# Queries of two batches projected in one matmul over 512 columns, in every second batch's turn

## The reference, cut to what matters

```python
q = jnp.einsum('oc,bct->bot', Wq, target) + bq[None, :, None]
k = jnp.einsum('oc,bcs->bos', Wk, source) + bk[None, :, None]
v = jnp.einsum('oc,bcs->bos', Wv, source) + bv[None, :, None]
dot = jnp.einsum('bhdt,bhds->bhts', q, k) / math.sqrt(HEAD_DIM)   # 16 heads of 8
mask = target_mask[:, :, :, None] * source_mask[:, :, None, :]
dot = mask * dot - (1.0 - mask) * NEG
amap = jax.nn.softmax(dot, axis=-1) * mask
out = jnp.einsum('bhts,bhds->bhdt', amap, v)
```

## Time and profile before

| | |
|---|---|
| median of 3 runs (lowest, highest) | 509.4 us (509.39, 510.41) |
| profiled execution, its own time | 509.36 us |
| its span, first to last instruction | 507.6 us |
| granted TensorE clock, mean of the span | 0.997 of full speed |
| PE busy, share of the span | 474.1 us, 93% |
| DVE busy | 381.3 us, 75% |
| ACT busy | 244.9 us, 48% |
| POOL busy | 230.1 us, 45% |
| the sixteen L1325 reduces of a batch, each | 0.68 us |

### The profile page before, as it was taken

One profiled execution on the slowest core, in us unless ns is written; L12 is line 12 of the kernel. 1 busy time (PEld: TensorE's weight loads), 2 busy tenths in 40 slices (PEclk: granted clock), 3 DMA queues, 4 the chain that ended last, 5 costly groups with the idle time before them and its releaser, 6 DMA issues. The chain is left out here.

```text
span 507.6 us, 10286 instructions
## 1 busy us (share of the span) xinstructions
PE 474.1 (93%) x3384; PEld 259.3 (51%) x3384; DVE 381.3 (75%) x765; ACT 244.9 (48%) x461; POOL 230.1 (45%) x319
## 2 busy tenths in 40 slices
PE   2998999998999999999999998998999999999993
PEld 2663664854733633343343333333445647788882
DVE  4989889899888789999999999998465633333321
ACT  2761232332232078889999998787412010233331
POOL 3736434154755355867677763213010660042433
PEclk9999999999999999999999999999999999999998
DMA  7750175002775116566566655300022224378843
GB/s 237 216 176 0 43 166 89 2 0 62 186 195 150 54 57 174 147 171 184 162 163 172 171 153 147 84 5 5 1 94 77 74 94 166 120 185 195 192 112 41
DMA packets 67256, 59.96 MB, mean 118 GB/s; under 512 B 10048, under 2 KB 62256, under 8 KB 67216
## 3 DMA queue, kind: packets, MB, share of 16 engines
q1 hardware_dynamic: 63712, 55.24, 39.6%
q0 software_dynamic: 3072, 4.21, 4.9%
q10 hardware_dynamic: 432, 0.00, 0.0%
HBM read 38.90 MB, written 22.50 MB: 121 GB/s over the span
## 5 line engine op out<-in xcount | busy, mean ns | idle before, releaser
L1325 DVE TENSOR_REDUCE MX<-psum 128x2 f32<-128x512 f32 x256 | 162.1, 682 | 10.0 <-PE psum L1190 8.4
L1374 ACT ACTIVATE HP<-psum 128x512 f32<-128x512 f32 x224 | 122.1, 602 | 28.9 <-PE psum L1205 26.4
L1190 PE MATMUL psum<-QKA 60*128 60x256 bf16 x512 | 81.3, 273 | 7.1 <-DVE MX L1325 5.6
L1205 PE MATMUL psum<-QKA 60*128 60x256 bf16 x512 | 81.1, 273 | 1.5 <-DMA QKA<-max_scr 1.0
L1291 PE MATMUL psum<-HP,VP 128*32 128x256 f32 x1024 | 81.8, 391 | 0.3 <-issue 0.2
L602 PE MATMUL psum<-space_a,space_w 128*128 128x512 f32 x160 | 73.1, 602 | 1.9 <-DVE HP L629 1.9
L1190 PEld LDWEIGHTS psum<-QKA 60*128 60x128 bf16 x512 | 31.6, 94 | 63.8 <-DVE MX L1325 44.6
L1966 POOL DMA_INDIRECT out_x<-OE,to_u x16 | 24.9, 1557 | 62.6 <-ACT OE L2001 60.1
L602 PEld LDWEIGHTS psum<-space_a,space_w 128*128 128x128 f32 x160 | 29.0, 190 | 36.5 <-issue 31.0
L2089 PE MATMUL psum<-XT,WE 128*128 128x256 f32 (+1 forms) x192 | 44.0, 379 | 0.9 <-ACT XT L1985 0.9
L199 PE MATMUL psum<-space_a,wsh 128*128 128x512 f32 (+1 forms) x96 | 43.6, 598 | 0.3 <-PEq L1497 0.3
(11 more groups left out here) (207 smaller groups left out, 767.3 us busy)
## 6 DMA issues: line engine op xcount, KB each, us to landing
QKA<-stack_scr SPq DMA_DIRECT2D x32, 480.0 KB, 4.5
stack_scr<-PARTS SPq DMA_DIRECT2D x32, 192.0 KB, 2.1
WE<-in_W SPq DMA_DIRECT2D x16, 352.0 KB, 4.0
stack_scr<-PARTS SPq DMA_DIRECT2D x32, 128.0 KB, 2.0
XD<-dispatched SPq DMA_DIRECT2D x8, 258.0 KB, 3.9
X<-in_x SPq DMA_DIRECT2D x4, 512.0 KB, 5.8
CTX<-in_ctx SPq DMA_DIRECT2D x4, 512.0 KB, 8.2
MB<-in_mask SPq DMA_DIRECT2D x16, 128.0 KB, 3.3
```

What stands on the lines that cost most here:

```text
L1190: return pe.matmul(to[:, tt * T:(tt + 1) * T], QKA[rows, k, 0, h, tt * P:(tt + 1) * P], QKA[rows, k, 1, h, :], start=True, stop=True)
L1205: return pe.matmul(to[:, (m % 2) * T:(m % 2 + 1) * T], QKA[rows, k, 1, h, st * P:(st + 1) * P], QKA[rows, k, 0, h, :], start=True, stop=True)
L1325: dve.tensor_reduce(MX[:, par, head_of(n), :], src[:, :].rearrange("p (a s) -> p a s", a=2), axis=AX.X, op=ALU.max).then_inc(a_red, 1)
L1374: act.activation(PT[:, i % 2, st, 2 * half:2 * half + 2, :].rearrange("p j t -> p (j t)"), TBK3[THIRDS[m]], ACT.Exp).then_inc(a_exp, 1)
```

## The change

Z3 gets two sides, and a new tile QS of two sides stands between the bank and QK. In turns 0 to 9, only the even turns have a query step: in step 3 POOL normalises batches b+6 and b+7, in step 6 PE projects both in one matmul over 512 columns into the whole of bank 7, in step 7 ACT takes 512 columns out. `act_qk` no longer waits until the rests of the batch before are done (a_rest), but until the masking of the batch two before has read its side of QS (a_masked). `pool_query` reads QS in place of QK. The transpose of maxima waits for a_x3 in every turn in addition to a_qk. The prologue keeps its single projections, in the new tiles.

```diff
-            Z3 = sbp("Z3", [P, T])
+            Z3 = sbp("Z3", [P, 2, T])
+            QS = sbp("QS", [P, 2, T])
...
+            def pe_proj_two(pe, g, k, to=bank[7]):
+
+                pe.wait_ge(a_z3, GB * g + k + 2)
+                pe.matmul(to[:, :], wq[:], Z3[:, :, :].rearrange("p b t -> p (b t)"), start=True, stop=True).then_inc(a_proj, 2)
...
             def act_qk(act, b, of=bank[7]):
 
                 act.wait_ge(a_proj, b + 1)
-                if later(b):
-                    act.wait_ge(a_rest, 2 * b)
-                act.activation(QK[:, 0:T], of[:, 0:T], ACT.Identity, bias=bqk[:, 0:1]).then_inc(a_qk, 1)
+                if b > 1:
+                    act.wait_ge(a_masked, b - 1)
+                act.activation(QS[:, b % 2, :], of[:, 0:T], ACT.Identity, bias=bqk[:, 0:1]).then_inc(a_qk, 1)
+
+            def act_qk_two(act, b, of=bank[7]):
+
+                act.wait_ge(a_proj, b + 2)
+                act.wait_ge(a_masked, b)
+                act.activation(QS[:, :, :].rearrange("p b t -> p (b t)"), of[:, :], ACT.Identity,
+                               bias=bqk[:, 0:1]).then_inc(a_qk, 2)
...
-                pool.tensor_tensor(QK[:, 0:T], QK[:, 0:T], MB[:, k, :], ALU.mult).then_inc(a_masked, 1)
+                pool.tensor_tensor(QK[:, 0:T], QS[:, k % 2, :], MB[:, k, :], ALU.mult).then_inc(a_masked, 1)
...
-                            if p == 7 and there(b, AHEAD_Z):
-                                act_qk(act, b + AHEAD_Z)
+                            if p == 7 and k % 2 == 0 and there(b, AHEAD_Z):
+                                act_qk_two(act, b + AHEAD_Z)
...
-                            if p == 3 and there(b, AHEAD_Z):
-                                pool_z3(pool, pch, b + AHEAD_Z)
+                            if p == 3 and k % 2 == 0 and there(b, AHEAD_Z):
+                                for side in range(2):
+                                    pool_z3(pool, pch, b + AHEAD_Z + side, side)
...
                             if p == 0 and there(b, 1):
                                 if there(b, AHEAD_Q):
                                     pe.wait_ge(a_qk, b + AHEAD_Q + 1)
-                                else:
+                                if later(b - 1):
                                     pe.wait_ge(a_x3, b - 1)
...
-                            if p == 6 and there(b, AHEAD_Z):
+                            if p == 6 and k % 2 == 0 and there(b, AHEAD_Z):
                                 if first(b):
                                     pe.wait_ge(a_nm, 2)
                                 else:
                                     pe.wait_ge(a_x3, b)
-                                pe_proj_q(pe, *at(g, k, AHEAD_Z))
+                                pe_proj_two(pe, *at(g, k, AHEAD_Z))
```

More of the change, by code:

```diff
@@ L687, in pe_proj_q @@
                 pe.wait_ge(a_z3, GB * g + k + 1)
-                pe.matmul(to[:, 0:T], wq[:], Z3[:], start=True, stop=True).then_inc(a_proj, 1)
+                pe.matmul(to[:, 0:T], wq[:], Z3[:, k % 2, :], start=True, stop=True).then_inc(a_proj, 1)
+            def pe_proj_two(pe, g, k, to=bank[7]):
+                pe.wait_ge(a_z3, GB * g + k + 2)
+                pe.matmul(to[:, :], wq[:], Z3[:, :, :].rearrange("p b t -> p (b t)"), start=True, stop=True).then_inc(a_proj, 2)
             def dve_z3(dve, b):
@@ L693, in dve_z3 @@
                     dve.wait_ge(a_proj, b)
-                dve.tensor_scalar(Z3[:], xb(b), mv3[:, bass.ds(b, 1), 0], rstd3[:, bass.ds(b, 1)], ALU.subtract, ALU.mult).then_inc(a_z3, 1)
+                dve.tensor_scalar(Z3[:, b % 2, :], xb(b), mv3[:, bass.ds(b, 1), 0], rstd3[:, bass.ds(b, 1)], ALU.subtract, ALU.mult).then_inc(a_z3, 1)
             def part_of(r):
@@ L1308, in pe_yo, with pool_z3 @@
                     last.then_inc(a_yo, 1)
-                def pool_z3(pool, pch, b):
+                def pool_z3(pool, pch, b, side):
                     pool.wait_ge(a_rstd, b // GB + 1 if isinstance(b, int) else NG)
-                    pool.wait_ge(a_proj, b)
-                    pch.do(pool.tensor_tensor(Z3[:], xb(b), mv3[:, bass.ds(b, 1), 0].broadcast_to([P, T]), ALU.subtract))
+                    pool.wait_ge(a_proj, b - side)
+                    pch.do(pool.tensor_tensor(Z3[:, side, :], xb(b), mv3[:, bass.ds(b, 1), 0].broadcast_to([P, T]), ALU.subtract))
                     pch.wait()
-                    pool.tensor_tensor(Z3[:], Z3[:], rstd3[:, bass.ds(b, 1)].broadcast_to([P, T]), ALU.mult).then_inc(a_z3, 1)
+                    pool.tensor_tensor(Z3[:, side, :], Z3[:, side, :], rstd3[:, bass.ds(b, 1)].broadcast_to([P, T]), ALU.mult).then_inc(a_z3, 1)
                 def dve_reduce(dve, g, k, n, SBK=None):
```

## The result

| | before | changed |
|---|---|---|
| median, first measurement | 509.41 us (509.26 to 510.41, 6 runs) | 512.36 us (511.50 to 513.42, 6 runs) |
| ratio to before | | 1.0055, interval 1.0040 to 1.0071 |
| profiled execution, its span | 509.36 us, 507.6 us | 513.09 us, 511.2 us |
| two later measurements of the changed kernel | 509.54, 509.50 us | 512.31 (511.63 to 513.08, 5 runs), 511.49 us (511.30 to 512.65, 5 runs) |

The change makes the kernel slower, by 0.55% in the first measurement; 511.1 us was forecast, with a range of 509.7 to 512.4 us that the 512.36 us meets by 0.04. The page of the changed kernel says as little on the cause as that of before: every engine is less busy and the span is longer.

The account below looks back on a forecast made before the run. The prediction took a ring of DVE's reduces and PE's chain as the bound. Five even turns at +0.42 us and four odd at -0.10 gave +1.70 us on 509.36, forecast as 511.1 us, range 509.7 to 512.4.

Parts of the forecast that it names:

- the sum: All turns 0 to 9: 5 x 0.42 - 4 x 0.10 = +1.70 us, giving 511.1 us, 0.33% slower.
- The bound: Attention turn: DVE's reduces and PE's chain form a ring, so a delay of head 15's reduce stays in the time.
- Even turns, 0.42 us: Turns 0, 2, 4, 6, 8: 256 more columns in two records on PE cost 0.42 us each, bounds 0.22 to 0.72.
- The rival that only head 15's 0.22 us gets through: Even turns: the delay is partly taken up, +0.7 us in all, 510.1 us; chance 0.12.
- the one of the cheap long matmul: PE's projection: longer matmul costs less than its columns, 0.12 us per even turn, 509.6 us; chance 0.05.
- The waits that I costed at nothing: Changed waits, such as the copy's for masking and PE's for a_x3, were taken to add 0 us.
- PE's a_x3 wait ahead of the transpose: Added wait before the transpose of maxima: costs nothing, as its addition ran in step 5 of the turn before.
- Odd turns, 0.10 us: Turns 3, 5, 7, 9: no query step saves 0.10 us each, bounds 0.07 and 0.12; turn 1 gives nothing.
- the 0.08 of the four reduces: DVE's last four reduces of a turn: 2.55 us with a projection, 2.47 without, so head 14 is 0.08 us late.
- the reading from the reciprocals, 0.12: Spacing of the once-a-turn reciprocal: 11.58 us with projection, 11.46 without, 0.12 us, loop and written-out turns mixed.
- The covers of ACT, POOL and SP: Slack for larger copy, doubled normalisation and later stores: ACT 0.56 us, POOL 0.52; all under 0.8, none shown to fail.
- The prologue: Before the turns: batch 3's copy no longer waits 1.33 us for a rest, but that reaches nobody; costed at nothing.

Follow-up runs that it names:

- half: Changed kernel with the even turns' matmul taking only the first 256 columns: 509.79 us.
- inc_one: Changed kernel with a_proj raised by 1 instead of 2 for each matmul of two queries, waiters counting accordingly: 511.24 us.
- sides: Changed kernel, its two-sided tiles and new waits kept, but one query normalised, projected and copied in every turn: 509.47 us, ratio to before 1.0004.
- gap_inc_one: Changed kernel with the two-query projection moved between heads 14 and 15 of step 7 and a_proj raised by 1: 509.89 us.
- parts_two: Changed kernel with two sides of PARTS, so ACT's split of batch b waits for the stores of batch b-2, not b-1: 511.69 us.

## Why the prediction was right, and where it was short

The mechanism was right and the sum was short: 1.70 us was forecast for the turns and 2.2 measured. That the first median of 512.36 us still lies in the range, by 0.04, is in part luck, since it holds about 0.7 us beside the turns that no term of the sum has.

- **The bound.** Right. The turn is a ring of DVE's reduces and PE's chain: with not an instruction less, moving the projection into PE's wait takes 0.77 us from the kernel before and 1.98 from the changed one. PE's busy share fell and the kernel became slower.
- **Even turns, 0.42 us.** The step held: 0.43 us for the columns, five times (`half`). The single projection filled the hole and stuck out by 0.07 us (a gap of 0.67 where 0.60 is on time), and all that was added came through. The rival that only head 15's 0.22 us gets through, and the one of the cheap long matmul, both fall.
- **The waits that I costed at nothing.** Here the sum was short. I let the projection follow the values and put the output's way ahead of it; in the loop it is released by DVE's addition L1348, which ends 0.13 us before it (at 211.93, the weights at 212.06), and the instruction that the increase by 2 brings stands just there. 4 x 0.09 = 0.36 us (`inc_one`). PE's a_x3 wait ahead of the transpose, which I did weigh, cost nothing (`sides`).
- **Odd turns, 0.10 us.** A little too much, and inside the bounds of 0.07 and 0.12: from head 15's reduce to that of the next turn, turns 3, 5, 7 and 9 are 0.07 or 0.08 us shorter than before, in the changed kernel and in `half` alike, and turn 1 is not, as forecast. It is the 0.08 of the four reduces; the reading from the reciprocals, 0.12, had mixed in the loop's own rhythm.
- **The sum.** 5 x 0.43 + 4 x 0.09 - 4 x 0.08 = 2.19 us against 2.23 to 2.25 measured from head 15's reduce to head 15's, and 1.70 forecast. Of the 0.5 us that were missing, the semaphore instruction is 0.36. The shortest executions show the same, 511.30 us for the changed kernel and 509.09 for the one before.
- **The covers of ACT, POOL and SP.** They held, but each is thin: POOL's second pair ends at 213.22, PE projects at 213.81; ACT's copy ends 0.47 us ahead of the transpose, 0.56 in the forecast; the key has no idle time left ahead of it and the split of the maxima has 0.45 of its 0.62 us.

```profile
212.61 0.61 POOL L1330 TENSOR_TENSOR Z<-Z,rstd 128x256 f32<-128x256 f32 x1 [0.17 <-POOL Z L1328]
...
216.00 0.72 POOL L738 TENSOR_TENSOR QK<-KR,MB 128x256 f32<-128x256 f32 x1
...
218.30 0.44 POOL L1426 TENSOR_TENSOR NP<-NM,zeros 32x128 bf16<-32x128 f32 x1 [0.45 <-ACT NM L1368]
```

- **The prologue.** Costed at nothing for the change, which `sides` bears out. That an execution can be 0.5 to 1.2 us longer there, or longer outside the span, was not in the sum, though the highest of the three times of before, 510.41, was 1.0 us above the others.

## What to carry to other kernels

Larger and fewer instructions on PE didn't help here, though PE was the busiest engine: two engines hand banks to each other in a ring, and what counts is how long one instruction stands between two hand-overs. Look for the step in which the faster engine waits for the slower one, and put the side work there, in pieces no longer than the wait: the same single projection, moved by one head, gave 0.17%, a third of it from turn 0. Two short instructions in two holes are better than one long one that sticks out of a hole, and an increase that needs an instruction of its own costs its 0.09 us exactly where its queue is being released (`inc_one`), and nothing where the queue waits anyway (`gap_inc_one`). Where a change costs 2 us of 510, compare one place of the traces, such as the turns here, and not medians alone.

## What the runs showed of the hardware that I had not expected

- In the loop, an increase of a semaphore by 2 on the matmul put an EVENT_SEMAPHORE of 51 ns into PE's queue, which made 0.09 us more from the release to the weight load; an increase by 1 did not.
- A copy of 128x512 fp32 with bias out of PSUM took 0.69 us (L719), a plain one 0.59 (L1394, L1381), one of 128x256 with bias 0.48 (L707).
- Around the start of a block, the place of one 16 KB code packet went with up to 1.8 us: where it came at 122.3 to 122.4 us SP stood 0.8 to 1.3 us longer between two DMA issues and the block started that much later; where it came at 125.9 a store landed 2 us later; nothing was late where it came at 126.6 to 126.9. That it is the cause is inferred from the traces, not tried.
- The device time of one execution can hold over 1 us more outside the span of its instructions than that of another (1.67 to 1.87 us in all executions of the kernel before, up to 3.01 in `parts_two`).
